# Edge stage of a graph layer: 48 places for gathered rows, tile scores in two places, softmax links between single weighings, and the open sums rescaled behind a chunk's second weighing

## The reference, cut to what matters

```python
el = jnp.einsum('nhf,hf->nh', feat_src, attn_l)
er = jnp.einsum('nhf,hf->nh', feat_dst, attn_r)
e = el[src] + er[dst]
e = jnp.where(e >= 0, e, NEG_SLOPE * e)
e_max = jax.ops.segment_max(e, dst, num_segments=N)
...
exp_e = jnp.exp(e - e_max[dst])
denom = jax.ops.segment_sum(exp_e, dst, num_segments=N)
a = exp_e / jnp.maximum(denom[dst], 1e-16)
msg = feat_v[src] * a[:, :, None]
rst = jax.ops.segment_sum(msg, dst, num_segments=N)
```

## Time and profile before

| | |
|---|---|
| median of 3 runs | 3391.83 us (3384.01 to 3405.29) |
| profiled execution | 3404.08 us, span 3402.2 us |
| PE busy | 2323.1 us, 68% |
| DVE busy | 1814.0 us, 53% |
| POOL busy | 1302.6 us, 38% |
| ACT busy | 1045.2 us, 31% |
| granted TensorE clock, mean | 0.817 |

### The profile page before, as it was taken

One profiled execution on the slowest core, in us unless ns is written; L12 is line 12 of the kernel. 1 busy time (PEld: TensorE's weight loads), 2 busy tenths in 40 slices (PEclk: granted clock), 3 DMA queues, 4 the chain that ended last, 5 costly groups with the idle time before them and its releaser, 6 DMA issues. The chain is left out here.

```text
span 3402.2 us, 50353 instructions
## 1 busy us (share of the span) xinstructions
PE 2323.1 (68%) x11245; PEld 1760.3 (52%) x11246; DVE 1814.0 (53%) x3898; ACT 1045.2 (31%) x2749; POOL 1302.6 (38%) x1406
## 2 busy tenths in 40 slices
PE   4999998565776777777776677776333339999400
PEld 3777776223555555555555455555333328888300
DVE  5444443687666666656655565564444334444433
ACT  0111111002443444444434343443533313333100
POOL 0000000301655555655555555561243352222244
PEclk8999998898888788888888887888555559999755
DMA  3122212644555555655555655663655634444576
GB/s 118 58 70 70 68 64 82 215 167 149 170 159 168 165 165 173 180 175 169 172 161 166 183 170 152 177 185 118 208 130 136 131 72 141 145 146 144 176 251 233
DMA packets 238376, 508.79 MB, mean 150 GB/s; under 512 B 50320, under 2 KB 76432, under 8 KB 238208
## 3 DMA queue, kind: packets, MB, share of 16 engines
q0 software_dynamic: 85936, 274.85, 27.8%
q1 hardware_dynamic: 134752, 196.94, 18.8%
q10 hardware_dynamic: 17520, 35.44, 3.2%
HBM read 394.73 MB, written 112.37 MB: 149 GB/s over the span
## 5 line engine op out<-in xcount | busy, mean ns | idle before, releaser
L637 POOL DMA_INDIRECT arena<-v_table,idx x832 | 879.9, 1058 | 834.2 <-PE ps L1575 575.9
L1575 PE MATMUL ps<-arena 128*128 128x260 f32 x3328 | 948.0, 433 | 0.7 <-DVE arena L1192 0.7
L1575 PEld LDWEIGHTS ps<-arena 128*128 128x128 f32 x3328 | 679.0, 215 | 121.9 <-issue 7.3
L776 ACT ACTIVATE arena<-ps x832 | 502.8, 604 | 442.9 <-issue 359.0
L1397 PE MATMUL ps<-arena 128*128 128x24 bf16 (+4 forms) x1994 | 396.0, 329 | 243.8 <-ACT arena L767 107.5
L1192 DVE TENSOR_TENSOR arena<-arena 128x512 f32<-128x512 f32 x832 | 537.2, 685 | 0.0
L1397 PEld LDWEIGHTS ps<-arena 128*128 128x128 f32 (+1 forms) x1994 | 261.4, 191 | 386.4 <-issue 159.9
L1402 PE MATMUL ps<-ident,arena 128*128 128x128 f32 x1128 | 213.9, 308 | 299.9 <-DVE arena L1270 242.8
L1402 PEld LDWEIGHTS ps<-ident,arena 128*128 128x128 f32 x1128 | 150.9, 160 | 321.9 <-DVE arena L1270 247.7
L767 ACT ACTIVATE arena<-arena 128x24 bf16 x832 | 180.5, 217 | 269.5 <-issue 189.5
L677 POOL DMA_INDIRECT arena<-xn_table,e_idx x105 | 99.3, 946 | 282.1 <-PE ps L1402 264.7
(11 more groups left out here) (263 smaller groups left out, 3584.3 us busy)
## 6 DMA issues: line engine op xcount, KB each, us to landing
y_table<-arena SPq DMA_DIRECT2D x105, 256.0 KB
arena<-local_table ACTq DMA_DIRECT2D x52, 512.0 KB
...
arena<-v_table,idx POOLq DMA_INDIRECT x832
...
```

What stands on the lines that cost most here:

```text
L637: pool.indirect_dma_start(vg[:, j % 2 * U + i, :], None, v_table, bass.IndirectOffsetOnAxis(ap=idx[:, j, i:i + 1], axis=0))\
L776: act.activation(halves(fin[:, bass.ds(room, DH)], HALF), halves(ps[:, bass.ds(room, 2 * D)], D)[:, :, 0:HALF], ACT.Copy).then_inc(s("act_ ...
L1575: return pe.matmul(sums[h], hot[:, i // V, i % V, :], vg[:, b * U + i, h * HALF:(h + 1) * HALF], start=False, stop=False)
```

## The change

The ring of rows gets 48 places (`RING` = 3 chunks), the softmax's index ring 6, and the loops go by laps of 6 chunks (the least common multiple of 2 and 3) after 4 peeled ones. `er_cur` has two places, filled three chunks ahead. The waits of the dependent links on VectorE are taken apart from the links (`past_link` ahead of an instruction, `linked` on the one before), and the links stand one or two at a time between single weighings instead of in five groups. `factored` goes from behind weighing 3 to behind weighing 0, `rescaled` to behind weighing 1. On TensorE the next chunk's first transpose (`turned_e`) goes ahead of the reopening of the sums, the others follow later steps; ScalarE's exponentials go from behind steps 5 and 8 to behind 6 and 10. Some buffers change places in SBUF. What is computed stays the same.

```diff
 DUMMY, ACC, PREP = 0, 2, 4
-BETWEEN = (6, 10, 14)
+BETWEEN = (7, 11, 14)
+RING, LAP, OPEN_CHUNKS = 3, 6, 4
...
-        hot_t = at(o, U * P // 2, dt=BF16); o += U * P // 2
-        locals_ = at(o, U * P, dt=BF16).rearrange("p (b n) -> p b n", b=2); o += U * P
+        vg = at(o, RING * U, DH); o += RING * U * DH
+        er_cur = at(o, U * 3 * H, dt=BF16).rearrange("p (b n) -> p b n", b=2); o += U * 3 * H
         pen = at(o, 2, P + 1); o += 2 * (P + 1)
-        assert o <= 26448, o
-        o = b_end
         e_buf = at(o, U, H); o += U * H
-
         t_fwd = at(o, P); o += P
         t_full = at(o, P); o += P
         m_t = at(o, P); o += P
+        assert o <= 26448, o
+        o = mix_end
+        hot = at(o, U // V, V, P); o += U * P
+        fin = at(o, 2 * D + DH); o += 2 * D + DH
+        hot_t = at(o, U * P // 2, dt=BF16); o += U * P // 2
+        locals_ = at(o, U * P, dt=BF16).rearrange("p (b n) -> p b n", b=2); o += U * P
         acc_kept = at(o, 2, HALF); o += DH
...
-            def values(c, j, r):
-                wait_past(pool, s("e_lin"), c, 3)
-                look_up(c + 1, (j + 1) % 4)
+            def values(n, k):
+                c, j, v = number(n, k), k % LAP, k % RING
+                wait_past(pool, s("e_lin"), c, LAP - 1)
+                look_up(c + 1, (j + 1) % LAP)
                 apart(pool, s("step_idx"), c + 1)
                 for i in range(U):
-                    if later(c, 2) and i % 2 == 0:
-                        apart(pool, s("step_mm"), c * U + (i + 2 - 2 * U))
-                    pool.indirect_dma_start(vg[:, j % 2 * U + i, :], None, v_table,
+                    if later(c, RING) and i % 2 == 0:
+                        apart(pool, s("step_mm"), c * U + (i + 2 - RING * U))
+                    pool.indirect_dma_start(vg[:, v * U + i, :], None, v_table,
                                             bass.IndirectOffsetOnAxis(ap=idx[:, j, i:i + 1], axis=0))\
-                        .then_inc(s(f"rows_in{j % 2}"), 16)
+                        .then_inc(s(f"rows_in{v}"), 16)
             look_up(0, 0)
-            turns(pool, values, NCH, 4)
...
+            def tile_scores(i, b, d, word):
+                last = act.activation(er_cur[:, b, i * 3 * H:(i + 1) * 3 * H], er_flat[:, bass.ds(d * (3 * H), 3 * H)], ACT.Copy)
                 if i % V == V - 1:
                     last.then_inc(s("er_set"), 1)
                 return next_tile(d, turn_of(word, i)) if i < U - 1 else d
...
-            def chunk(c, b, r, own):
+            def chunk(n, k):
+                c, b = number(n, k), (k + 1) % 2
                 more = not (isinstance(c, int) and c == NCH - 1)
-                ahead = not (isinstance(c, int) and c >= NCH - 2)
-                (d, word), (d2, word2) = own[0], own[-1]
+                ahead = not (isinstance(c, int) and c >= NCH - 3)
+                (d, word), = chunk_places(ENGINE.Activation, c, 1)
                 if ahead:
+                    (d2, word2), = chunk_places(ENGINE.Activation, c + 3, 1)
                     act.wait_ge(s("er_mm"), c + 2)
                 for i in range(U):
                     if ahead:
-                        d2 = tile_scores(i, d2, word2)
+                        d2 = tile_scores(i, b, d2, word2)
...
-                    if i == 5:
+                    if i == 6:
                         factor(c + 1)
-                    elif i == 8:
-                        weights(c + 1, 1 - b)
-                        if not (isinstance(c, int) and c >= NCH - 3):
-                            chunk_in(c + 3, 1 - b)
+                    elif i == 10:
+                        weights(c + 1, (k + 1) % RING)
+                        if ahead:
+                            chunk_in(c + 3, b)
...
+            for c, (d, word) in enumerate(chunk_places(ENGINE.Activation, 0, 3)):
+                if c == 2:
+                    act.wait_ge(s("er_mm"), 1)
                 for i in range(U):
-                    d = tile_scores(i, d, word)
+                    d = tile_scores(i, c % 2, d, word)
...
-            def link_b(ins, c, k):
+            def linked(ins):
                 ins.then_inc(s("prep_link"), 1)
+
+            def past_link(c, k):
                 apart(dve, s("prep_link"), c * NL + (k + 1))
 
             def of_steps(col):
...
-            def scored(c, b, r):
+            def summed_parts(c):
                 dve.wait_ge(s("er_mm"), c + 1)
-                link_b(dve.tensor_reduce(e_buf, spread.rearrange("p (s i h) -> p s h i", s=U, i=3), AX.X, ALU.add), c, 0)
-                dve.wait_ge(s(f"rows_in{b}"), 16 * U * (r + 1))
-                link_b(dve.tensor_tensor(e_halves, e_halves, score_cols(b), ALU.add), c, 1)
+                linked(dve.tensor_reduce(e_buf, spread.rearrange("p (s i h) -> p s h i", s=U, i=3), AX.X, ALU.add))
+
+            def both_ends(c, v, r):
+                past_link(c, 0)
+                dve.wait_ge(s(f"rows_in{v}"), 16 * U * (r + 1))
+                linked(dve.tensor_tensor(e_halves, e_halves, score_cols(v), ALU.add))
+
+            def leaked(c):
+                past_link(c, 1)
                 dve.scalar_tensor_tensor(e_flat, e_flat, NEG_SLOPE, e_flat, ALU.mult, ALU.max).then_inc(s("e_lin"), 1)
 
-            def run_max(c, b):
+            def max_up(c, b):
                 dve.wait_ge(s("ev_tp"), c + 1)
-                link_b(dve.tensor_tensor_scan(t_fwd, pen[:, b, 0:P], prep[:, 0:P], -BIG, ALU.add, ALU.max), c, 2)
-                link_b(dve.tensor_tensor_scan(t_full[:, ::-1], pen[:, b, 1:P + 1][:, ::-1], t_fwd[:, ::-1], -BIG, ALU.add, ALU.max), c, 3)
...
+            def chunk(n, k):
+                c, v = number(n, k), k % RING
                 more = not (isinstance(c, int) and c == NCH - 1)
-                n, q = 1 - b, (r if b == 0 else r + 1)
+                b, v_next, r_next = (k + 1) % 2, (k + 1) % RING, lap_round(n, k + 1, RING)
                 for i in range(U):
                     if i % V == 0:
                         found(c * U + i, i)
                     if i == 0:
                         dve.wait_ge(s("p_exp"), c + 1)
-                    step(i, b)
-                    if i == 3 and later(c, 1):
+                    step(i, v)
+                    if i == 0 and later(c, 1):
                         factored(c)
+                    if i == 1 and later(c, 1):
                         rescaled(c)
                     if not more:
                         continue
-                    if i == 4 and not (isinstance(c, int) and c == NCH - 2):
-                        turned_hot(c + 2, b, r + 1)
+                    if i == 0:
+                        summed_parts(c + 1)
+                    elif i == 1:
+                        both_ends(c + 1, v_next, r_next)
+                    elif i == 2:
+                        leaked(c + 1)
+                    elif i == 4:
+                        max_up(c + 1, b)
                     elif i == 5:
-                        scored(c + 1, n, q)
-                    elif i == 7:
-                        run_max(c + 1, n)
+                        max_down(c + 1, b)
+                    elif i == 6:
+                        if not (isinstance(c, int) and c == NCH - 2):
+                            turned_hot(c + 2, k % 2, lap_round(n, k + 2, 2))
+                        outer_ends(c + 1)
+                    elif i == 8:
+                        links_up(c + 1)
                     elif i == 9:
-                        linked(c + 1)
+                        links_down(c + 1)
+                    elif i == 10:
+                        moved(c + 1)
                     elif i == 11:
-                        joined_max(c + 1, n)
+                        picked_links(c + 1)
+                    elif i == 12:
+                        own_links(c + 1)
+                        carried(c + 1)
                     elif i == 13:
-                        shifted(c + 1, n)
+                        joined_up(c + 1, b)
+                    elif i == 14:
+                        joined_down(c + 1, b)
+                    elif i == 15:
+                        shifted(c + 1, v_next)
             dve.wait_ge(s("mx_out"), NT)
             dve.memset(halves(ps[:, DUMMY * D:(DUMMY + 2) * D], D)[:, :, 0:HALF], 0.0).then_inc(s("dummy_set"), 1)
             turned_hot(0, 0, 0)
-            scored(0, 0, 0)
-            run_max(0, 0)
-            linked(0)
-            joined_max(0, 0)
+            summed_parts(0)
+            both_ends(0, 0, 0)
+            leaked(0)
+            max_up(0, 0)
+            max_down(0, 0)
+            outer_ends(0)
+            links_up(0)
...
-            def chunk(c, b, r, own):
-                word = own[0][1]
+            def chunk(n, k):
+                c, v = number(n, k), k % RING
+                (_, word), = chunk_places(ENGINE.PE, c, 1)
                 more = not (isinstance(c, int) and c == NCH - 1)
                 ahead = not (isinstance(c, int) and c >= NCH - 2)
+                if more:
```

(17 more changed lines are left out.)

111 lines of the change are left out of this document (65 added, 46 removed).

## The result

The changed kernel takes 3517.2 us (median; 3513.7 to 3525.9) where the one before takes 3395.7 beside it: ratio 1.036, 95% interval 1.032 to 1.040. It is 121 us slower, against a forecast of 3165 (range 3060 to 3290) and a chance of 0.06 for slower. That holds on the chip of this comparison and for its kind. On a chip of another kind the same two kernels take 3196.1 and 3307.3 us, ratio 0.967 (0.963 to 0.970), 111 us faster (run after_again). Both results need an explanation, and so does the difference between them.

A forecast was written before the change was run, and what follows sets the result against it. The edge stage was taken as a ring of waits, no engine full, 30.0 us a chunk. Terms -138 - 29 - 20 + 20 - 64 + 4 = -227 from 3404.1 gave 3177, or 3165 us on the median's footing; range 3060 to 3290.

The forecast's parts named there:

- Third place for rows: VectorE's edge-stage wait for gathered rows at L1140 would end: -138 us, bounds 0 and -138.
- Tile scores in two places: TensorE's 106.6 us wait for ScalarE's tile scores would end, worth VectorE's 29.3 us at L1134: -29 us.
- Late tile ends: TensorE's waits for ScalarE's copies at tile ends would shrink from 131.8 us: -64 us, bounds 0 and -94.
- Links singly and the order around them: Undisturbed chain of waits around one chunk would shorten from 21.1 to 20.7 us: -20 us over 50 chunks.
- The transposition and the clock: Transpose ahead of TensorE's reopening lengthens its idle boundary, adding low-clock steps: +20 us, bounds 0 and +170.
- The cover of 0.3 to 0.9 us: Margin by which VectorE's answers would come before TensorE, running through its steps after reopening, needs them.
- Prologue: Before the edge stage, 16 more tile scores delay the first factor: +4 us; extra gathers in the mix stage: 0.
- Sum: All terms together, mostly in the edge stage: -227 us, 3165 us on the median's footing, 25.4 us a chunk.
- the hold: VectorE's weighings hold up POOL's gathers for their whole length: pitch 1.94 us, 3467 us; chance 0.03.
- the first rival: Less gain: ScalarE stays late at tile ends or low clock every other chunk; 3230 to 3245, both near 3290; chance 0.18.
- the low clock: TensorE drops to its low clock at every reopening and stays there: 35.7 us a chunk, 3677 us; chance 0.03.
- No change: Waits at VectorE's rescaling take back the gains, 4.6 us a chunk: 3392 us, plus or minus 34; chance 0.04.

The follow-up runs named there:

- sum_behind_blocks: Changed kernel with previous order except rescaling behind weighing 2, sum right behind it, both ends behind 3, leaky ReLU behind 4; 3136.6 us, 0.957 of before, calm chip.
- old_both: Changed kernel's places, previous order, 512 KB transfer behind step 1, row gathers of chunks 1 and 2 held until mix stage ends; 3092.2 us, 0.936, calm chip.
- old_rows_gated: Changed kernel's places with previous order, row gathers of chunks 1 and 2 held until the mix stage ends; 3112.1 us, 0.942 of before, calm chip.
- ring2: Changed kernel with 32 places for rows instead of 48, new order kept; 3624.0 us, 1.065 of before, late chip.
- old_rescale1: Changed kernel's places with previous order, but rescaling behind weighing 2 instead of 4; 3367.5 us, 0.992 of before, late chip.
- reopen_first: Changed kernel with TensorE's transposition of the next chunk's logits back behind step 1; 3502.1 us, 1.030 of before, late chip (1.034 on another).
- sum_behind: Changed kernel with transposition behind step 1, sum behind the rescaling, both ends behind weighing 3, leaky ReLU behind 4; 3437.5 us, 1.011 of before, late chip.
- old_order_again: Changed kernel's 48 row places and two tile-score places, every engine's order as before; 3122.2 us, 0.944 of before, calm chip.

## Why the prediction was wrong, and what of it was right

On the calm chip, with nothing late, its steps can be read one by one. Stage, VectorE's waits, TensorE's wait at tile ends, and the reopening's products (min/median/max ns), for the kernel before (before_again):

```profile
840.00:2224.80 1384.80, 1090.29 (x4872) 788.99 (x4872) 921.87 (x2099) 613.85 (x1687) 833.19 (x837) 0.86 0.62 182
```

```profile
DVE arena L1140 <- DMA arena<-v_table,idx: 191.7, 50, 7.7
DVE arena L1192 <- PE ps L1565: 139.6, 50, 6.6
DVE r_all L1181 <- PE ps L1397: 51.3, 25, 6.1
DVE g_fwd L1153 <- PE ps L1397: 13.1, 10, 2.2
```

```profile
PE ps L1565 <- ACT arena L776: 76.3, 47, 3.3
```

```profile
L1600 PE MATMUL ps<-arena,ident x204: 382/383/803, 840.0 to 2225.6; 128*128 128x260 f32 x102
```

and for the changed kernel (after_again), with TensorE's waits:

```profile
853.00:2112.80 1259.80, 1053.58 (x4873) 782.01 (x4872) 875.90 (x2096) 606.24 (x1665) 956.46 (x823) 0.88 0.69 198
```

```profile
DVE arena L1153 <- PE ps L1472: 133.4, 49, 4.9
DVE r_all L1225 <- PE ps L1472: 97.1, 44, 6.5
DVE g_fwd L1181 <- PE ps L1472: 69.5, 47, 4.5
DVE picked L1195 <- PE ps L1472: 43.9, 49, 2.5
...
DVE arena L1158 <- DMA arena<-v_table,idx: 5.2, 3, 2.5
```

```profile
PE ps L1620 <- DVE arena L1162: 153.9, 50, 5.5
PE ps L1640 <- ACT arena L787: 51.7, 47, 2.1
```

```profile
L1678 PE MATMUL ps<-arena,ident x204: 382/641/676, 853.0 to 2113.5; 128*128 128x260 f32 x102
```

- **Third place for rows, -138.** Right in mechanism: the wait goes from 138.3 us to 0.0 late and from 191.7 to 5.2 calm.
- **Tile scores in two places, -29.** TensorE's wait for them is gone in both pairs. The 29.3 us at L1134, by which it was priced, went to 0.0 late; on the calm chip only 0.5 stood there before.
- **Late tile ends, -64.** Right on the late chip, 131.8 to 73.0 (42.9 + 30.1), longest 7.3; on the calm one there was less to gain, 76.3 to 51.7.
- **Links singly and the order around them, -20.** This step failed. It priced the move of the sum as work, -0.47 us, and kept 0.9 us from the closing product to the rescaling's end. But with the instruction moved its wait, for the last score product of the chunk before, to a place ahead of the rescaling and behind one weighing. The time from the closing product to the rescaling's end, in the mean over the chunks, is 2.0 us calm and 8.1 late, where the kernel before has 0.9 and 2.0. The row is L1153 with 133.4 us, 2.7 a chunk; what left the rescaling (139.6 to 1.6) is there. VectorE's work did get shorter, 922 to 876 us, and it is 916 in sum_behind_blocks, so most of these 46 us of busy time are saved by the single links.
- **The transposition and the clock, +20, one more low stretch in every eighth chunk.** This failed too. The boundary was to grow by 1.0 us, from 0.9 to 1.9; it grew from 1.5 to 3.5 calm and from 3.1 to 9.5 late. The reopening's product has a median of 641 ns in the changed kernel where it has 383 before, on the calm chip. Read in the first microsecond of each of the 51 reopenings, the granted clock is 0.50 at 36 in the changed kernel and at 12 before; one in eight more would have been 6 more. VectorE waits longer for TensorE's later answers: in front of g_fwd 69.5 us instead of 13.1, and in front of picked 43.9 instead of 4.2, together 96 us, half of what the rows gave. The cover of 0.3 to 0.9 us that the working named was used up there. How much of this is the late transposition, the lower clock or the place of the single links, no run separates. In front of r_all it waits 97.1 instead of 51.3, but that goes with the rescaling's earlier place: in sum_behind_blocks, where the reopening is at 383 ns again, it is more.

```profile
DVE r_all L1225 <- PE ps L1465: 117.4, 46, 7.5
```

On the late chip the reopening's median is 641 too, but there it was 641 already; the granted clock is 0.50 at 49 of 51 reopenings and was at 36:

```profile
L1678 PE MATMUL ps<-arena,ident x204: 382/641/642, 877.1 to 2468.7; 128*128 128x260 f32 x102
```

- **Prologue, +4.** It is +13 calm and +29 late. The working took 16 more gathers in the mix stage for nothing because POOL idles. It has idle time there, and yet the stage ends later. The same 100 us of the mix stage, before and changed (columns as in the earlier trace rows):

```profile
600.00:700.00 100.00, 56.20 (x164) 25.75 (x164) 70.24 (x84) 7.68 (x20) 25.39 (x28) 0.90 0.63 206
```

```profile
600.00:700.00 100.00, 49.20 (x121) 22.93 (x119) 51.38 (x63) 5.76 (x15) 43.62 (x48) 0.70 0.68 217
```

28 and 48 POOL instructions, and VectorE's 84 fell to 63, TensorE's 164 to 121, while the transfers' share rose from 0.63 to 0.68. That the loads of that stage stand behind the gathers' transfers is argued from this. On a calm chip old_both and old_rows_gated, which hold gathers back, start the edge stage at 837.5 and 840.8, and the calm kernels that do not hold them at 851 to 856; on a late chip the gathers do not explain all 29, by ring2 above.
- **Sum.** On calm chips 25.2 us a chunk, where 25.4 was forecast; but before has 27.7 there, not 30.0. So the agreement is luck: the gain is 2.5 a chunk, not 4.6, and 111 us, not 227. The calm stage is 125 us shorter, of which VectorE's idle time gives 79 (463 to 384) and its busy time 46; the later start takes 13 back. Two small figures of the working are off and bear on nothing: the hold loses above a pitch of 1.84 us, not 1.9, and 3245 as the upper end of the first rival has no sum behind it (both its terms give 3230).
- **What was not in the working at all** is the late kind's loss. The prediction saw 78 us of waits without a cause at the multiply ("remote" 46.9, "issue" 31.0 in the earlier trace rows), and set them aside because nothing of the change aimed at them. On calm chips none of these "remote" waits is there, so they belong to the lateness. Before, VectorE had four rows weighed when it stopped; now one. 46.9 + 45.1 us of "remote" became 418. That fewer rows weighed ahead is why the lateness grew is argued; old_rescale1, which stops behind two, lost only some 0.005, so it is not the count alone. From reopen_first to sum_behind 0.020 to 0.023 of before came back, on two chips, when the sum's wait was moved behind the rescaling.
- **Signs named ahead.** On the late chip, rows near 0, tile scores gone, tile ends 50 to 75, clock 0.81 and gathers 1.151 us came as said. POOL's wait for TensorE did not go: 386.8 us, before 381.2, since at 31.8 us a chunk POOL is ahead again; only on the calm chip is it down to 48. The multiply and r_all were to keep 250 to 360 us and have 112; "over 450" was to mean wrong, and with the sum, which took their place, it is 560. No wait at a tile end was to be over 4 us, and the longest is 7.3.
- **The rivals.** Of those that said slower, neither is it: the low clock asked for a clock under 0.75 and it is 0.81, the hold for gathers of 1.94. "No change" had the mechanism that came nearest, the rescaling taking back what the rows gave, and named 4.6 us a chunk for it. On the late chip the multiply, r_all and the sum have 560 us where the first two had 317, which is 4.9 a chunk, and g_fwd and picked stand 109 us longer on top of it.
- **The hold.** The rival gave gathers of 1.94 us, 3467. The Trainium skill, SBUF — State Buffer, section Who interferes with whom, has the rule beside it: a VectorE instruction with two inputs in SBUF contends with a GpSimd instruction that reads SBUF; for descriptor writing the page infers that it needs only the other interface. The gathers average 1.151 and 1.213 us in the changed kernel. In old_order_again, with VectorE busy 925 of 1190 us instead of 876 of 1260, they take less:

```profile
L648 POOL DMA_INDIRECT arena<-v_table,idx x832 | 880.8, 1059 | 503.8 <-PE ps L1640 302.6
```

1.059 us. VectorE's busy share does not set the length of a gather here, and a hold of a whole weighing is not seen. The traces agree with the page's inference and not with the rule as a price of gathers.

For comparison old_order_again, where the boundary is 1.2 us and the reopening has 383 ns (row above):

```profile
853.20:2043.10 1189.90, 1003.61 (x4873) 735.34 (x4873) 924.88 (x2100) 613.14 (x1673) 841.34 (x820) 0.94 0.72 209
```

```profile
DVE arena L1236 <- PE ps L1630: 127.2, 48, 6.6
DVE r_all L1225 <- PE ps L1462: 43.1, 20, 5.3
DVE arena L1166 <- PE ps L1610: 22.0, 11, 5.9
```

Its clock is 0.94 instead of 0.88, TensorE is busy 1004 us instead of 1054 for the same products, and all of VectorE's waits for TensorE sum to 209 us instead of 375. In sum_behind_blocks the reopening is at 383 ns again:

```profile
L1669 PE MATMUL ps<-arena,ident x204: 382/383/802, 851.5 to 2087.7; 128*128 128x260 f32 x102
```
